# Attention with an adjacency mask on one core: a block's sums leave PSUM as one product, and one low part of GpSimd's waits for a minimum

## The reference

```python
scores = einsum('nd,md->nm', x, ks)
scores = leaky_relu(scores, negative_slope=0.2)
scores = where(adj > 0, scores, -9e15)
attn = softmax(scores, axis=1)
return layernorm(x + einsum('nm,md->nd', attn, ks))     # eps 1e-5
```

## Time and profile before

| | |
|---|---|
| time, median of 3 runs | 1547.73 us (1546.6 to 1548.18) |
| time of the profiled execution | 1547.7 us |
| its span, first to last instruction | 1545.8 us |
| mean granted TensorE clock | 0.997 |
| busy: ACT | 1470.7 us (95%) |
| chain that ended last | PE 75%, issue 9%, DVE 9%, ACT 5% |
| HBM traffic | 190 GB/s over the span |

### The profile page before, as it was taken

One profiled execution on the slowest core, in us unless ns is written; L12 is line 12 of the kernel. 1 busy time (PEld: TensorE's weight loads), 2 busy tenths in 40 slices (PEclk: granted clock), 3 DMA queues, 4 the chain that ended last, 5 costly groups with the idle time before them and its releaser, 6 DMA issues.

```text
span 1545.8 us, 43366 instructions
## 1 busy us (share of the span) xinstructions
PE 1504.8 (97%) x16828; PEld 1416.8 (92%) x16828; DVE 1512.0 (98%) x1820; ACT 1470.7 (95%) x1872; POOL 1434.8 (93%) x1241
## 2 busy tenths in 40 slices
PE   6699999999999999999999999999999999999997
PEld 5599999999999999999999999999999999999997
DVE  7999999999999999999999999999999999999996
ACT  6999999999999999999999999999999999999996
POOL 4999999999999999999999999999999999999986
PEclk9999999999999999999999999999999999999999
DMA  9865666656666656666655656656665656565620
GB/s 370 267 194 188 204 200 196 195 190 195 193 192 191 202 188 193 196 194 192 200 188 190 192 184 193 195 183 193 193 189 190 198 177 197 191 194 188 192 83 8
DMA packets 107132, 296.02 MB, mean 191 GB/s; under 512 B 10800, under 2 KB 40240, under 8 KB 106928
## 3 DMA queue, kind: packets, MB, share of 16 engines
q1 hardware_dynamic: 106928, 293.25, 58.9%
HBM read 289.01 MB, written 4.19 MB: 190 GB/s over the span
## 4 chain that ended last, share of the span: by engine, by line
PE 75%; issue 9%; DVE 9%; ACT 5%; POOL 1%; DMA 1%; SPq 0%; DVEq 0%; POOLq 0%; ACTq 0%
PE weighted L850 21%; PE scores L802 11%; PE scores L804 11%; PE scores L803 11%; PE weighted L866 7%; PE weighted L862 7%; PE weighted L864 7%; DVE running L679 4%; DVE ring L698 3%; ACT ring L504 2%; DVE ring L665 1%; ACT pt_hi L511 1%; DMA adj_sb<-in_adj 1%; POOL kt_lo L372 0%; PE floors L833 0%
## 5 line engine op out<-in xcount | busy, mean ns | idle before, releaser
L405 POOL TENSOR_TENSOR ring<-ring,floor 128x768 f32<-128x768 f32 x494 | 698.9, 1415 | 47.7 <-ACT floor L531 47.7
L410 POOL TENSOR_TENSOR pt_lo<-ring,pt_hi 128x512 f16<-128x512 f32 (+1 forms) x512 | 658.4, 1286 | 22.5 <-ACT pt_hi L511 19.4
L665 DVE SCALAR_TENSOR_TENSOR ring<-adj_sb,scores 128x1024 f32<-128x1024 int32 x512 | 620.3, 1211 | 3.9 <-ACT scores L497 3.6
L497 ACT ACTIVATE scores<-scores,shrink 128x1024 f32<-128x1024 f32 x512 | 553.6, 1081 | 50.4 <-PE scores L804 45.7
L504 ACT ACTIVATE ring<-ring,lift 128x1024 f32<-128x1024 f32 x512 | 583.0, 1140 | 2.3 <-DVE ring L698 2.3
L802 PE MATMUL scores<-xt_hi,kt_hi 128*128 128x256 f16 x2048 | 558.7, 273 | 21.4 <-DVE ring L665 17.0
L804 PE MATMUL scores<-xt_hi,kt_lo 128*128 128x256 f16 x2048 | 559.2, 273 | 0.0
L803 PE MATMUL scores<-xt_lo,kt_hi 128*128 128x256 f16 x2048 | 558.9, 273 | 0.0
L679 DVE TENSOR_TENSOR running<-ring,running 128x1024 f32<-128x1024 f32 x448 | 547.3, 1222 | 0.1
L850 PE MATMUL weighted<-k_rows,ring 128*128 128x129 f32 x3472 | 471.6, 276 | 2.5 <-DVE y L719 1.4
L850 PEld LDWEIGHTS weighted<-k_rows,ring 128*128 128x128 f32 x3472 | 426.6, 192 | 14.5 <-ACT ring L504 8.4
(11 more groups left out here) (78 smaller groups left out, 561.8 us busy)
## 6 DMA issues: line engine op xcount, KB each, us to landing
adj_sb<-in_adj SPq DMA_DIRECT2D x512, 512.0 KB, 3.5
ring<-in_ks_t SPq DMA_DIRECT2D x8, 512.0 KB, 7.7
x_row<-in_x SPq DMA_DIRECT2D x32, 128.0 KB, 3.9
out<-normed SPq DMA_DIRECT2D x32, 128.0 KB, 3.7
x_probe<-in_x_t SPq DMA_DIRECT2D x29, 128.0 KB, 3.5
xt_raw<-in_x_t SPq DMA_DIRECT2D x29, 128.0 KB, 4.4
ring<-in_ks SPq DMA_DIRECT2D x12, 128.0 KB, 7.6
k_rows<-in_ks SPq DMA_DIRECT2D x12, 128.0 KB, 4.6
```

The source lines that it names most:

```text
L405: nc.gpsimd.tensor_tensor(here, here, below, ALU.subtract).then_inc(gap_ready, 1)
L410: nc.gpsimd.tensor_tensor(pt_lo[:, g % PARTS, 0:QUAD - whole, :], ring[:, g % RING, whole:, :], pt_hi[:, g % PARTS, 0:QUAD - whole, :], AL ...
L665: nc.vector.scalar_tensor_tensor(ring[:, g % RING, :, :], adj_sb[:, g % ADJS, :, :], 0.0, scores[:, g % 2, :, :], ALU.is_le, ALU.subtract)\
```

## The change

There are three edits in the blocks below the last.

1. `finish` forms the reciprocal of the raw sum of exponentials, then one product of both sides' sums with it, from PSUM into a new SBUF tile `ratio`. The scale of the denominator is gone; its inverse, `unscale_rows`, is the scalar of the two multiply-adds, which are now in a function of their own, `residual`, and read `ratio` and `x_row`. PE waits for `ratio_ready` in place of `y_ready`.
2. In the slot with a finish the order on DVE becomes: subtraction, finish, mask, minimum, residual. In the last block finish and residual stay together at the slot's start.
3. `low_part` on POOL waits in each fourteenth group (index 13 of 16) for the first minimum of the block two after, if there is such a block.

```diff
+    HELD = GROUPS + AT_GAP - AT_PART
...
-        denom = sb("denom", [P, SIDES], F32)
+        ratio = sb("ratio", [P, SIDES, D], F32)
...
+        unscale_rows = f32_column(unscale, K_ALL)
...
             def low_part(g):
+                first = (g // GROUPS + 2) * GROUPS + 1
+                if g % GROUPS == HELD and first < ALL:
+                    pool.wait_ge(running_ready, least_count(first))
                 wait_high(pool, g)
...
             def finish(b):
-                at = b % 2
+
                 total = sums(b)[:, 0:SIDES * LANES].rearrange("p (j w) -> p j w", j=SIDES)
                 dve.wait_ge(weighted_ready, GROUPS * (b + 1))
-                nc.vector.tensor_scalar(denom[:, :], total[:, :, ONES], scale_rows, None, ALU.mult).then_inc(denom_ready, 1)
-                dve.wait_ge(denom_ready, b + 1)
+                wait(dve, ratio_ready, b)
+                nc.vector.reciprocal(recip[:, :], total[:, :, ONES]).then_inc(recip_ready, 1)
+                dve.wait_ge(recip_ready, b + 1)
                 wait(dve, y_ready, SIDES * b)
-                nc.vector.reciprocal(recip[:, :], denom[:, :]).then_inc(recip_ready, 1)
+                nc.vector.tensor_tensor(ratio[:, :, :], total[:, :, 0:D],
+                                        recip[:, :].unsqueeze(2).to_broadcast([P, SIDES, D]), ALU.mult)\
+                    .then_inc(ratio_ready, 1)
+
+            def residual(b):
+                at = b % 2
+                dve.wait_ge(ratio_ready, b + 1)
                 dve.wait_ge(xrow_loaded[at], 16 * (b // 2 + 1))
-                dve.wait_ge(recip_ready, b + 1)
                 wait(dve, normed_ready, SIDES * b)
                 for j in range(SIDES):
-                    nc.vector.scalar_tensor_tensor(y[:, j, :], total[:, j, 0:D], recip[:, j:j + 1],
-                                                   x_row[:, at, j, :], ALU.mult, ALU.add,
-                                                   accum_out=y_sum[:, j:j + 1]).then_inc(y_ready, 1)
+                    nc.vector.scalar_tensor_tensor(y[:, j, :], ratio[:, j, :], unscale_rows, x_row[:, at, j, :],
+                                                   ALU.mult, ALU.add, accum_out=y_sum[:, j:j + 1]).then_inc(y_ready, 1)
...
-                b = whole(s, AT_FINISH)
-                if b is not None:
-                    finish(b)
+                ended = whole(s, AT_FINISH)
+                if ended is not None:
+                    if ended < BLOCKS - 1:
+                        gap(s - AT_GAP + 1)
+                    finish(ended)
+                    if ended == BLOCKS - 1:
+                        residual(ended)
...
-                    if g is not None and early == (g % GROUPS > 0):
+                    if g is not None and early == (g % GROUPS > 0) and (ended is None or ended == BLOCKS - 1):
                         gap(g)
                 g = group(s, 1)
                 if g is not None and 0 < g % GROUPS < LAST:
                     least(g)
+                if ended is not None and ended < BLOCKS - 1:
+                    residual(ended)
...
                 if q == 0 and b < BLOCKS - 1:
-                    wait(pe, y_ready, SIDES * b)
+                    wait(pe, ratio_ready, b)
```

More of the change, by code:

```diff
@@ L177, in adj_attention_layernorm @@
         part_lo_ready = sem("part_lo_ready")
-        denom_ready = sem("denom_ready")
+        ratio_ready = sem("ratio_ready")
         prob_ready = sem("prob_ready")
```

## The result

| | before | changed |
|---|---|---|
| time, median | 1547.85 us (1546.6 to 1548.18, 4 runs) | 1565.26 us (1563.82 to 1566.28, 4 runs) |
| ratio, 95% interval | | 1.0113 (1.0096 to 1.0131) |
| time of the profiled execution | 1547.7 us | 1565.8 us |
| its span | 1545.8 us | 1563.9 us |

What follows compares the result with a forecast made beforehand. DVE was taken to bound the kernel once its loop with PE is cut. Terms: -6.0 (waits) + 1.8 (product) + 27 (meeting) = +22.8 us, from 1547.7 to 1570.5 us, range 1543.4 to 1578.

Steps and rivals of the forecast that it cites:

- DVE bounds once the loop with PE is cut: Steady block: PE alone needs about 46.2 us, DVE about 46.23; cutting their mutual waits gains at most 0.25 a block.
- The product: Finish on DVE: one 128x256 product replaces the denominator, 1.13 us instead of 1.07, +1.8 us over 30 blocks.
- The waits of the loop go: DVE's wait before the denominator and PE's for y_ready vanish: 0.2 us on 30 blocks, -6.0 us.
- The subtraction moved ahead costs nothing: DVE's subtraction, one mask earlier, fills the 0.24 us that DVE idled: cost 0.
- The hold costs nothing by itself: POOL's held low part makes POOL 1.02 us late, within its customers' room, 1.33 at the tightest of the rest.
- The hold moves a low part under the multiply-add: POOL's later low part, 1101.85 to 1103.01, starts 0.13 us before DVE's first multiply-add at 1101.98 and blocks it.
- The price, 0.90 on 30 blocks: DVE's first multiply-add loses 0.90 us in each of 30 held blocks: +27 us, bounds 0 and +36.
- Rival (a): DVE's multiply-adds pass POOL's low part, which is blocked itself with its lateness covered: 1543.5 us; chance 0.2.
- Rival (b): Multiply-adds pass, POOL some 1.75 us late, PE waits at the 768-wide low part: 1544 to 1553 us; chance 0.15.
- Rival (c): DVE starts first, POOL takes its turn between the multiply-adds, the second waits 1.16 us: 1576.5 us; chance 0.1.

Runs made afterwards that it cites:

- run with a PSUM operand: Changed kernel, but up to block 29 the multiply-adds add a row of floors in PSUM in place of x_row in SBUF: 1541.51 us, ratio 0.9961.
- the pair of 905.63: Multiply-adds in the run that moved the changed kernel's multiply-adds to just ahead of the block's first minimum and dropped POOL's hold: 1552.78 us, ratio 1.0035.
- run one mask later: Changed kernel with the multiply-adds moved behind the mask of the next slot: 1565.36 us, ratio 1.0117.
- run one minimum earlier: Changed kernel with the two multiply-adds ahead of the slot's minimum instead of behind it: 1592.37 us, ratio 1.0290.
- run with the two repairs: Against the no-hold kernel with multiply-adds just ahead of the first minimum: hold in three blocks only, last block but one finishes earlier; 1547.86 us, ratio 1.0000.

## Why the prediction was right

The direction and the mechanism are confirmed; the size was 17.4 us where 22.8 was forecast. By the steps:

- **DVE bounds once the loop with PE is cut.** Right, though PE's own loss was misread: from 1100.05 to 1100.35 it is 0.30 - 0.11 = 0.19, not 0.26, which puts PE alone at 46.28 and not at 46.2. No term of the sum rests on it. The run with a PSUM operand has blocks of 46.26 us, where 46.23 + 0.06 was worked out, and a time of 1541.5 with nothing but DVE's own work in the block.
- **The product.** The reciprocal is followed by the product after 0.21 and the mask after 0.34; with 0.28 and 0.27 for undisturbed multiply-adds that is 1.10 where 1.13 was laid out and 1.07 was spent before. The product itself is 0.42 long, where its nearest row was 0.41. The multiply-add with two SBUF tensors is neither faster nor slower than the one with PSUM when nothing disturbs it (0.34 against 0.35). The Trainium skill's two fixed costs (VectorE: DVE Perf Modes, § The TRN2 errata) would by that page's estimate have made each 0.06 shorter; the runs do not agree, for the means are 346 ns with the hold undone and 349 ns before.
- **The waits of the loop go.** Right, and sized a little low. Gain of stalls and cost of work together were put at -4.2; the run with the PSUM operand shows -6.1.
- **The subtraction moved ahead costs nothing.** Right: it fills DVE's former idle time, and the reciprocal starts at 1112.14 without a wait.
- **The hold costs nothing by itself.** Right: 1547.37 against 1547.62. The layout had POOL 1.02 late.
- **The hold moves a low part under the multiply-add.** Right, and the margin too: POOL was put first by 0.13, and in the blocks shown it is first by 0.09 in the changed kernel and by 0.12 with the PSUM operand. That is a narrow margin. That the meeting falls the same way in every steady block is no luck, since both chains start anew at the same minimum. That a layout of fifteen steps put the right one of the two first by 0.13 owes something to luck. DVE reaches the multiply-add 13.18 after the first minimum; 13.21 was laid out.
- **The price, 0.90 on 30 blocks.** This is the term that was mis-sized. A meeting costs 1.15 - 0.27 = 0.88, and there are 29 of them (the multiply-adds over 1 us in the trace), 25.5 us of DVE's time. (In the last block, the thirtieth that is held, the pair passes, with 0.35.) Of this 23.8 reach the end, against 27 forecast. With the 1.9 above this is nearly the whole difference between 22.8 and 17.4.

The layout's answer for the rivals was weaker. Rival (a), the pair passes although the low part is held, was made by no run: where the pair passes, with the hold undone, the minimum loses 0.37 a block, and that belongs to the missing hold. What the prediction held against (a), that the second multiply-add would then meet the waiting low part, is borne out by the pair of 905.63, which came first and lost 1.6. Rival (b) named a path that is real, but saw it at one low part only and gave it up to 9 us for a lateness of 1.75; in the run one mask later POOL was some 2.2 late, PE waited at three low parts, and it cost some 24 against the run with the PSUM operand. What exactly 1.75 would cost no run shows. Rival (c), POOL's turn between the two, did not happen in the changed kernel, since POOL waits for `y` behind its low part; it happens as soon as POOL has work ready.

## What to carry to other kernels

Taking a result out of PSUM early gives PE its bank back, but the instruction that reads the copy has one more SBUF operand, and with two of them it excludes a POOL instruction that reads SBUF. Before such a step is moved, lay POOL's timeline under it, behind every wait that is added to POOL: a delay that costs its own customers nothing can push another instruction into the place where DVE has two SBUF operands. When two short DVE instructions of this kind follow each other, leave POOL idle for both, for it takes its turn in between.

## What the runs showed of the hardware

- A 128x128 multiply-add on DVE with two SBUF tensors is blocked by a running POOL instruction just as the 128x1024 minimum is: 1.22 us instead of 0.35, and it ends 0.15 us after POOL's does. The Trainium skill (SBUF — State Buffer, § Who interferes with whom) says of any VectorE instruction with two SBUF inputs that it contends with a GpSimd instruction that reads SBUF, without telling short from long, and this trace now agrees for a short one. With one of the tensors in PSUM both run at full speed (0.34 and 1.16).
- The two engines alternate when both have instructions ready. In the run one minimum earlier the order is subtraction, multiply-add, low part, multiply-add; the second loses 0.9 although DVE's instructions stood directly behind each other. A lead at the first of them did not help the second either (905.63: 0.34, 905.90: 1.90).
- A lead of POOL's of 0.08 to 0.10 us decides the meeting alike in 28 blocks of the changed kernel: the multiply-adds met are between 1.21 and 1.24 us long. In the first, where the lead is 0.21, it is 1.10. In the run with the two repairs 0.05 and 0.06 are enough.
